# Ternary weight making in an 8-core attention and BitLinear kernel: moved ahead of the second projection batch, from VectorE to ScalarE, and through device memory

## The reference

```python
xn = layernorm(x)
# attention part, per sequence
q, k, v = xn @ Wq, xn @ Wk, xn @ Wv
gq = sum_s(q * softmax(q * SCALE, -1))
p  = gq * k
gk = sum_s(p * softmax(p * SCALE, -1))
attn = q + (gk * v) @ Wr
# feed-forward part: 8-bit activations, ternary weights
scale_w = 1 / clip(mean(abs(w)), 1e-5)
wq = clip(round(w * scale_w), -1, 1) / scale_w        # for w_gate, w_up, w_down
ffn = bitlinear(silu(bitlinear(xn, w_gate)) * bitlinear(xn, w_up), w_down)
y = x + attn + ffn
```

## Time and profile before

| | us |
|---|---|
| timed runs, all (2) | 5378.8 and 5394.5, median 5386.6 |
| profiled execution, its own time | 5350.1 |
| its span, slowest core (core 5) | 5348.5 |
| quickest cores (1 and 3) | 5265.2 |
| DVE busy | 3306.7 (62%) |
| PE busy | 2379.1 (44%) |
| ACT busy | 1899.7 (36%) |
| POOL busy | 60.7 (1%) |

### The profile page before, as it was taken

The page is one execution under the profiler, slowest core; times in us unless marked ns, Lnnn a source line. Parts: engine busy times, 40 slices in busy tenths (PEclk is TensorE's granted clock), DMA queues, the critical chain, the costliest instruction groups (busy, mean ns, idle before and its releaser), DMA issues.

```text
span 5348.5 us, 37244 instructions; the slowest of 8 cores (5265.2 to 5348.5 us)
## 1 busy us (share of the span) xinstructions
PE 2379.1 (44%) x10182; PEld 1037.9 (19%) x10182; DVE 3306.7 (62%) x3647; ACT 1899.7 (36%) x2114; POOL 60.7 (1%) x117
## 2 busy tenths in 40 slices
PE   1443413444100044434444444444444228888888
PEld 0111101111000021212212112112112014433333
DVE  3777657777557767787777777777777701111111
ACT  1222213333000035565565555555555501111111
POOL 1000000000000000000000000000000000000000
PEclk9666656666555567777767777677677558877777
DMA  4222203332233310000000000000000132221121
GB/s 86 79 77 69 75 0 104 108 108 83 84 114 118 113 38 12 20 20 20 20 10 20 20 20 20 20 10 20 20 20 18 34 102 89 85 89 71 73 82 40
DMA packets 85712, 296.02 MB, mean 55 GB/s; under 512 B 9728, under 2 KB 9728, under 8 KB 77312
## 3 DMA queue, kind: packets, MB, share of 16 engines
q1 hardware_dynamic: 32256, 134.23, 7.2%
q10 hardware_dynamic: 39168, 117.46, 6.7%
q0 software_dynamic: 14080, 41.95, 3.2%
HBM read 209.72 MB, written 92.27 MB: 56 GB/s over the span
## 4 chain that ended last, share of the span: by engine, by line
DVE 37%; PE 28%; ACT 17%; issue 9%; DMA 7%; DVEq 1%; ACTq 1%; POOL 0%; SPq 0%; POOLq 0%
ACT rA L685 10%; DVE fl L688 9%; PE PB L626 6%; DVE lh L372 6%; PE PC L629 5%; PE PC L826 5%; PE PA L826 5%; DVE lh L369 3%; PE PB L812 3%; DVE stat L647 3%; PE PT L796 2%; ACT z_hqT L800 2%; DMA wdT_sb<-swdT 2%; ACT f_g L635 2%; DVE fl L694 1%
## 5 line engine op out<-in xcount | busy, mean ns | idle before, releaser
L626 PE MATMUL PB<-wgT_sb,f_xiT 128*128 128x512 bf16 x2048 | 863.7, 422 | 1252.3 <-ACT f_g L635 1185.1
L685 ACT ACTIVATE rA<-fl,cbias 128x1024 bf16<-128x1024 f32 x512 | 588.0, 1148 | 439.0 <-DVE fl L675 284.6
L688 DVE SCALAR_TENSOR_TENSOR fl<-rA,fl 128x1024 f32<-128x1024 bf16 x512 | 627.3, 1225 | 162.9 <-ACT rA L685 162.5
L694 DVE SCALAR_TENSOR_TENSOR fl<-rB,fl 128x1024 f32<-128x1024 bf16 x512 | 625.0, 1221 | 14.6 <-ACT rB L691 12.8
L691 ACT ACTIVATE rB<-fl,cbias 128x1024 bf16<-128x1024 f32 x512 | 586.9, 1146 | 16.9 <-DVE fl L694 15.0
L626 PEld LDWEIGHTS PB<-wgT_sb,f_xiT 128*128 128x128 bf16 x2048 | 218.2, 107 | 1573.4 <-issue 1385.6
L629 PE MATMUL PC<-wuT_sb,f_xiT 128*128 128x512 bf16 x1024 | 468.9, 458 | 0.0
L629 PE MATMUL PA<-wuT_sb,f_xiT 128*128 128x512 bf16 x1024 | 389.4, 380 | 0.0
L635 ACT ACTIVATE f_g<-PB,cgv 128x512 f32<-128x512 f32 x256 | 167.9, 680 | 543.6 <-PE PC L629 531.6
L372 DVE TENSOR_TENSOR lh<-lh,lh 128x1024 f32<-128x1024 f32 x256 | 313.7, 1225 | 27.3 <-DVE lh L369 0.9
L487 PE MATMUL P<-p_w,p_rep 128*128 128x512 bf16 x64 | 37.5, 585 | 596.6 <-DVE p_w L484 566.5
(11 more groups left out here) (129 smaller groups left out, 3480.1 us busy)
## 6 DMA issues: line engine op xcount, KB each, us to landing
shqT<-f_hq SPq DMA_DIRECT2D x32, 1024.0 KB, 4.5
z_hq<-shqT SPq DMA_DIRECT2D x32, 1024.0 KB, 5.5
wf<-wgT ACTq DMA_DIRECT2D x48, 512.0 KB, 3.7
wf<-wuT ACTq DMA_DIRECT2D x48, 512.0 KB, 3.6
wf<-wdT ACTq DMA_DIRECT2D x48, 512.0 KB, 3.6
xbuf<-x SPq DMA_DIRECT2D x32, 512.0 KB, 4.3
sacc<-accs SPq DMA_DIRECT2D x32, 512.0 KB, 2.9
z_acc<-sacc ACTq DMA_DIRECT2D x32, 512.0 KB, 6.3
```

The source lines that it names most:

```text
L626: last = te.matmul(gps, lhsT, wgT_sb[:, k * I + jj * 512:k * I + (jj + 1) * 512], start=(k == 0), stop=(k == 7))
L685: o("scalar", (lambda j=j, scale=scale: lambda s: s.activation(rA[:], fl1[:], AF.Relu, scale=scale, bias=cbias[:, j:j + 1]))(), reads=[fl1 ...
L688: o("vector", (lambda cc=cc, op1=op1: lambda v: v.scalar_tensor_tensor(fl1[:], rA[:], cc, fl1[:], ALU.min, op1))(), reads=[rA_b], writes=[ ...
L694: o("vector", (lambda cc=cc, op1=op1: lambda v: v.scalar_tensor_tensor(fl2[:], rB[:], cc, fl2[:], ALU.min, op1))(), reads=[rB_b], writes=[ ...
```

## The change

passA is done in batch 0's projections altogether, with six items a step in place of two, and the three means follow there. passB then runs earlier: one item behind each of batch 0's softmax tiles (16 items), and five items behind each step of batch 1's projections (80 items in 16 steps; the last two steps have none). Batch 1's second softmax has no passB any more.

What an item does is changed as well. Two ACT instructions compute sign(w*scale - 0.5) into tstA and sign(w*scale + 0.5) into one of two buffers tern_st, both bf16; DVE adds them in bf16, which gives -2, 0 or 2 (the factor 0.5 goes into the scales, L534 of before). The result goes to device memory for all three matrices, on POOL for even items and ACT for odd ones; loads are on ACT for even items and POOL for odd ones, as before. The pieces stand in the order gate, up, down in place of down, up, gate.

The up and gate weights are loaded into SBUF from there, on SP, in 1 MB pieces: 14 of 16 are issued ahead of batch 1's second softmax, and the last two, whose place wgT_hi overlaps that softmax's buffers, behind it. The gate weights lie in two buffers for that, wgT_lo and wgT_hi. In the down stage only addresses change (wdT_sb and the tiles beside it trade places).

```diff
+    swgT_h = nc.dram_tensor("swgT", [D, I], BF16, kind="Internal").ap()
+    swuT_h = nc.dram_tensor("swuT", [D, I], BF16, kind="Internal").ap()
...
+    bm5, bm5_b = sb("bm5", [128, 1], F32, 19.875)
+    bp5, bp5_b = sb("bp5", [128, 1], F32, 19.9375)
...
-    wf32_t, wf32_bl = sb("wf32", [128, 2 * D], F32, 197.125, nbuf=2)
+    wf32_t, wf32_bl = sb("wf32", [128, 2 * D], F32, 197.375, nbuf=2)
     wf32 = [wf32_t[:, i * D:(i + 1) * D] for i in range(2)]
-    wabs, wabs_b = sb("wabs", [128, D], BF16, 205.25)
+    wabs, wabs_b = sb("wabs", [128, D], BF16, 205.375)
...
-    ternA, ternA_b = sb("ternA", [128, D], F32, 127.5)
-    ternA2, ternA2_b = sb("ternA2", [128, D], F32, 37.125)
-    wgT_sb, wgT_sb_b = sb("wgT_sb", [128, 8 * I], BF16, 69.125)
...
+    tstA, tstA_b = sb("tstA", [128, D], BF16, 191.375)
+    tern_st_t, tern_st_bl = sb("tern_st", [128, 2 * D], BF16, 193.375, nbuf=2)
+    tern_st = [tern_st_t[:, i * D:(i + 1) * D] for i in range(2)]
+    wgT_lo, wgT_lo_b = sb("wgT_lo", [128, 6 * I], BF16, 69.125)
+    wgT_hi, wgT_hi_b = sb("wgT_hi", [128, 2 * I], BF16, 117.125)
...
+    wdT_sb, wdT_sb_b = sb("wdT_sb", [128, 32 * D], BF16, 133.125)
...
+            if drip is not None:
+                drip()
+
+    passB = ([("wg", k) for k in range(32)] + [("wu", k) for k in range(32)]
+             + [("wd", k) for k in range(32)])
+
+    def emit_passB(idx):
+        nm, k = passB[idx]
+        slot = idx % 2
+        if nm == "wd":
+            src = wdT_h[k * 128:(k + 1) * 128, :]
+            dst = swdT_h[k * 128:(k + 1) * 128, :]
+            ridx, dst_b = 10, swdT_b[k]
+        else:
+            w_hh = wgT_h if nm == "wg" else wuT_h
+            s_hh = swgT_h if nm == "wg" else swuT_h
+            src = w_hh[(k // 4) * 128:(k // 4 + 1) * 128, (k % 4) * D:(k % 4 + 1) * D]
+            dst = s_hh[(k // 4) * 128:(k // 4 + 1) * 128, (k % 4) * D:(k % 4 + 1) * D]
+            ridx = 8 if nm == "wg" else 9
+            dst_b = (swgT_b if nm == "wg" else swuT_b)[k]
+        o("scalar" if idx % 2 == 0 else "gpsimd",
+          (lambda src=src, slot=slot:
+           lambda s: s.dma_start(out=wf32[slot], in_=src))(),
+          writes=[wf32_bl[slot]], dma=True)
+        o("scalar", (lambda slot=slot, ridx=ridx: lambda s: s.activation(
+            tstA[:], wf32[slot], AF.Sign, scale=wstat[:, ridx:ridx + 1],
+            bias=bm5[:, 0:1]))(),
+          reads=[wf32_bl[slot], wstat_b, bm5_b], writes=[tstA_b])
+        o("scalar", (lambda idx=idx, slot=slot, ridx=ridx: lambda s: s.activation(
+            tern_st[idx % 2], wf32[slot], AF.Sign, scale=wstat[:, ridx:ridx + 1],
+            bias=bp5[:, 0:1]))(),
+          reads=[wf32_bl[slot], wstat_b, bp5_b], writes=[tern_st_bl[idx % 2]])
+        o("vector", (lambda idx=idx: lambda v: v.tensor_tensor(
+            tern_st[idx % 2], tern_st[idx % 2], tstA[:], ALU.add))(),
+          reads=[tstA_b, tern_st_bl[idx % 2]], writes=[tern_st_bl[idx % 2]])
+        o("gpsimd" if idx % 2 == 0 else "scalar",
+          (lambda idx=idx, dst=dst: lambda s: s.dma_start(
+              out=dst, in_=tern_st[idx % 2]))(),
+          reads=[tern_st_bl[idx % 2]], writes=[dst_b], dma=True)
+
+    pb_i = [0]
+
+    def drip_passB(n):
+        for _ in range(n):
+            if pb_i[0] < len(passB):
+                emit_passB(pb_i[0])
+                pb_i[0] += 1
+
+    p1_batch(0, 6)
...
-    o("vector", lambda v: v.tensor_scalar_mul(wstat[:, 12:15], wstat[:, 4:7], -1.0),
+    o("vector", lambda v: v.tensor_scalar_mul(wstat[:, 12:15], wstat[:, 4:7], 0.5),
...
-    passB = ([("wd", k) for k in range(32)] + [("wu", k) for k in range(32)]
-             + [("wg", k) for k in range(24)] + [("wg", k) for k in range(24, 32)])
...
-        tA, tA_b = (ternA2, ternA2_b) if (nm == "wg" and k >= 24) else (ternA, ternA_b)
-        o("vector", (lambda slot=slot, ridx=ridx, tA=tA: lambda v: v.tensor_scalar(
-            tA[:], wf32[slot], wstat[:, ridx:ridx + 1], 0.5, ALU.mult, ALU.is_ge))(),
-          reads=[wf32_bl[slot], wstat_b], writes=[tA_b])
-        o("vector", (lambda slot=slot, ridx=ridx, oap=oap: lambda v: v.tensor_scalar(
-            oap, wf32[slot], wstat[:, ridx:ridx + 1], -0.5, ALU.mult, ALU.is_le))(),
-          reads=[wf32_bl[slot], wstat_b], writes=[tgt_b])
-        o("vector", (lambda oap=oap, tA=tA: lambda v: v.tensor_tensor(
-            oap, oap, tA[:], ALU.subtract))(),
-          reads=[tA_b, tgt_b], writes=[tgt_b])
-        if nm == "wd":
-            o("scalar", (lambda k=k: lambda s: s.dma_start(
-                out=swdT_h[k * 128:(k + 1) * 128, :], in_=wabs[:, 0:D]))(),
-              reads=[wabs_b], writes=[swdT_b[k]], dma=True)
-
...
-    for i2, t in enumerate(range(NTB, NT)):
+    for t in range(NTB):
         p2_tile(t)
-        drip_passB(6, 88)
+        drip_passB(1)
+    o("vector", lambda v: v.tensor_copy(gk_s[:, 0:D], gkbc[:]),
+      reads=[gkbc_b], writes=[gk_s_b])
+    o("vector", lambda v: v.memset(gqbc[:], 0.0), writes=[gqbc_b])
+    o("vector", lambda v: v.memset(gkbc[:], 0.0), writes=[gkbc_b])
+
+    p1_batch(1, 0, drip=lambda: drip_passB(5))
+    drip_passB(len(passB))
+
+    def wu_load(kk):
+        o("sync", (lambda kk=kk: lambda s: s.dma_start(
+            out=wuT_sb[:, kk * I:(kk + 1) * I],
+            in_=swuT_h[kk * 128:(kk + 1) * 128, :]))(),
+          reads=[swuT_b[kk * 4 + j] for j in range(4)],
+          writes=[wuT_sb_b], dma=True)
+
+    def wg_load(kk):
+        tgt, tb = (wgT_lo, wgT_lo_b) if kk < 6 else (wgT_hi, wgT_hi_b)
+        c0 = kk * I if kk < 6 else (kk - 6) * I
+        o("sync", (lambda kk=kk, tgt=tgt, c0=c0: lambda s: s.dma_start(
+            out=tgt[:, c0:c0 + I],
+            in_=swgT_h[kk * 128:(kk + 1) * 128, :]))(),
+          reads=[swgT_b[kk * 4 + j] for j in range(4)],
+          writes=[tb], dma=True)
+
+    for kk in range(8):
+        wu_load(kk)
+    for kk in range(6):
+        wg_load(kk)
+    for t in range(NTB, NT):
+        p2_tile(t)
     o("vector", lambda v: v.tensor_copy(gk_s[:, D:2 * D], gkbc[:]),
       reads=[gkbc_b], writes=[gk_s_b])
-    drip_passB(len(passB), len(passB))
+    wg_load(6)
+    wg_load(7)
...
-                last = te.matmul(gps, lhsT,
-                                 wgT_sb[:, k * I + jj * 512:k * I + (jj + 1) * 512],
-                                 start=(k == 0), stop=(k == 7))
+                wg_sl, _ = wg_ap(k, jj * 512, (jj + 1) * 512)
+                last = te.matmul(gps, lhsT, wg_sl, start=(k == 0), stop=(k == 7))
```

More of the change, by code:

```diff
@@ L128, in build_nc @@
     swdT_b = [Buf("swdT%d" % k) for k in range(32)]
+    swgT_b = [Buf("swgT%d" % k) for k in range(32)]
+    swuT_b = [Buf("swuT%d" % k) for k in range(32)]
     allocs = []
@@ L203, in build_nc, with wg_ap @@
     p2_rep, p2_rep_b = sb("p2_rep", [128, 128], BF16, 127.15625)
-    ternA, ternA_b = sb("ternA", [128, D], F32, 127.5)
-    ternA2, ternA2_b = sb("ternA2", [128, D], F32, 37.125)
-    wgT_sb, wgT_sb_b = sb("wgT_sb", [128, 8 * I], BF16, 69.125)
+    tstA, tstA_b = sb("tstA", [128, D], BF16, 191.375)
[3 more added lines that the diff above has]
+    wgT_hi, wgT_hi_b = sb("wgT_hi", [128, 2 * I], BF16, 117.125)
     wuT_sb, wuT_sb_b = sb("wuT_sb", [128, 8 * I], BF16, 133.125)
+    def wg_ap(k, off0, off1):
+        if k < 6:
+            return wgT_lo[:, k * I + off0:k * I + off1], wgT_lo_b
+        return wgT_hi[:, (k - 6) * I + off0:(k - 6) * I + off1], wgT_hi_b
     f_xi_t, f_xi_bl = sb("f_xi", [128, 2 * D], BF16, 37.125, nbuf=2)
@@ L263, in build_nc @@
     o("vector", lambda v: v.memset(halfv[:], 0.5), writes=[halfv_b])
+    o("vector", lambda v: v.memset(bm5[:], -0.5), writes=[bm5_b])
+    o("vector", lambda v: v.memset(bp5[:], 0.5), writes=[bp5_b])
     for j in range(8):
@@ L494, in p2_tile, with p1_batch @@
               reads=[P7_b], writes=[gkbc_b])
-    def p1_batch(bi, rate):
+    def p1_batch(bi, rate, drip=None):
         base = bi * NTB
@@ L509, in p1_batch @@
             drip_passA(rate)
-    p1_batch(0, 2)
-    for t in range(NTB):
-        p2_tile(t)
-    o("vector", lambda v: v.tensor_copy(gk_s[:, 0:D], gkbc[:]),
-      reads=[gkbc_b], writes=[gk_s_b])
-    o("vector", lambda v: v.memset(gqbc[:], 0.0), writes=[gqbc_b])
-    o("vector", lambda v: v.memset(gkbc[:], 0.0), writes=[gkbc_b])
-    p1_batch(1, 4)
+            if drip is not None:
+                drip()
+    passB = ([("wg", k) for k in range(32)] + [("wu", k) for k in range(32)]
+             + [("wd", k) for k in range(32)])
@@ L573, in build_nc @@
-    pb_i = [0]
-    def drip_passB(n, limit):
-        for _ in range(n):
-            if pb_i[0] < limit:
-                emit_passB(pb_i[0])
-                pb_i[0] += 1
-    for i2, t in enumerate(range(NTB, NT)):
-        p2_tile(t)
-        drip_passB(6, 88)
+    for t in range(NTB):
+        p2_tile(t)
+        drip_passB(1)
+    o("vector", lambda v: v.tensor_copy(gk_s[:, 0:D], gkbc[:]),
+      reads=[gkbc_b], writes=[gk_s_b])
+    o("vector", lambda v: v.memset(gqbc[:], 0.0), writes=[gqbc_b])
```

(2 more changed lines are left out.)

41 lines of the change are left out of this document (11 added, 30 removed).

## The result

The changed kernel takes **5657.6 us** (median of 11 runs) against 5310.4 us before (10 runs): the ratio is 1.0644, with a 95% interval of 1.0582 to 1.0706. Of 5310 us that is 342, and the medians differ by 347; the forecast sum was +359. The profiled execution took 5687.3 us.

A forecast was written before the change was run, and what follows sets the result against it. DVE, nearly gapless, was taken to set the pace of a batch 1 projection step, with ACT slack. Terms +59 + 11 + 649 - 360 = +359 on the profiled 5350.1 us, plus 18 for timed runs, gave 5727 us; range 5590 to 5840.

The forecast's parts named there:

- The ring of five items: Batch 1's projections: each item runs load, two Signs, add, store, with nothing of the next starting early; +649 us.
- the 8.7 and 8.8: Batch 1's projections, inside a step: an odd item costs 8.7 us, an even item 8.8, from add to add.
- the 71 and 80: Batch 1's projections: steps alternate near 71 and 80 us, as they begin with an even or odd item.
- 5.22: Batch 1's projections: microseconds from an even item's load issue on ACT until its data are used.
- The last softmax: Batch 1's second softmax, without passB: 517.3 us falls to 157.8, including 13 us to the first gate matmul; -360.
- passA: Batch 0's projections, six items a step instead of two: 39 us for late ACT plus 20 for slower weight loads, +59.
- The rate part: Batch 0's projections: two more items than the four shown make ACT 2.8 us late in 14 steps, 39 us.
- the first two steps slow the loading of wq, wk and wv: Start of batch 0's projections: eight more passA loads each slow a projection weight load by 2.5 us, +20.
- The first softmax: Batch 0's second softmax: one passB item per tile costs only DVE's add, 0.69 us (upper end 1.23), 16 times: +11.
- Rival (c), tables: Sign is not in ACT's loaded function table; extra table loads cost 41 us, at worst 82; about 5790; chance 0.09.
- (a): Batch 1's projections: loads hidden, only Signs and add remain, 3.2 us an item, 222 instead of 649; 5300 us; chance 0.06.
- (b): Batch 1's projections: ACT's work fits under DVE's quantisation, leaving 80 adds, 55 us; total -235, 5133 us; chance 0.04.

The follow-up runs named there:

- the experiment: Kernel before with passA at six items a step, all in batch 0's projections, and the means ahead of batch 0's second softmax: 5314.8 against 5281.7 us.

## Why the prediction held, point by point

- **The ring of five items (+649, measured +637)** is shown: parting loads from stores, from either side, brings 245 to 362 us. The 8.56 us between adds answer to the 8.7 and 8.8, and steps of 72.4 and 79.8 us (from 957.20, 1029.61 and 1109.44) to the 71 and 80; over the batch those that begin even take 67 to 72 us and those that begin odd 77 to 82.
- **Inside the ring** the numbers were less good than the sum, and that they agree in the mean is luck: inside a step an even item took 8.05 us and an odd one 9.08 (means of 32 each), where I had 8.8 and 8.7. An ACT load took 4.40 us from issue to use where I had 5.22, a POOL load 4.64 where I had 4.45, and it was issued 0.73 behind the start of the store where I had 0.53.
- **Where the 5.22 came from**: it was read at a place where a second load and a store were under way beside the load. ACT's loads in that softmax of before took 4.96 us to landing where both were (median of 15) and 3.72 where neither was (22); inside the change's steps, with a store alone beside them, 3.85 (32). This is a sorting of loads and no experiment. The Trainium skill, DMA: Bandwidth & Descriptors, on queues, rings and completion order, says that the increment of a DMA's semaphore lands after the earlier writes of that DMA engine. I had read it as making every load behind a store late; the 3.85, against 3.57 for the eight ACT loads here with no store beside them, show 0.3 us of that (0.6 as means), not the 1.6 that I took. What held the loads was that they were issued late.
- **The last softmax (-360, measured -361)** held. From its last add to the first gate matmul it took 14.5 us where I had 13, by another path than I had: the first exposed 1 MB load landed 5.9 us after its issue at 2214.61, and then the second load (2220.55 to 2226.69) and f_xi's (2220.96 to 2227.41) went side by side. I had put them one behind the other, and f_xi's took 6.5 us where it took 2.6 in the kernel before, with no weights under way.
- **passA (+59, measured +32 without the means)** is the term that failed. The rate part held: L442 comes 2.4 us late in a step as a mean of 14 instead of 2.8, and the experiment gives +33 in all. The part "the first two steps slow the loading of wq, wk and wv", +20, does not exist: the first Kst cast comes at 129.0 us, before at 131.0. Twelve passA loads lie in that stretch in place of four, and the last of the 24 weight loads landed at 115.7 us, before at 117.4. The slower load of the earlier trace rows was one of few, with the last load of wq (46.16 to 51.63) beside it too, and I had multiplied its excess by eight. ACT around the end of a late step, where the sixth item (431.81) pushes the casts and L442 behind DVE's maximum, which began at 431.64:

```profile
431.81 1.06 ACT L309 ACTIVATE wabs<-wf 128x1024 bf16<-128x1024 f32 x1 [2.62 <-DMA wf<-wuT]
...
435.28 0.20 ACT L442 ACTIVATE stat<-stat 128x1 f32<-128x1 f32 x1 [0.51 <-ACT v L434]
```

- **The first softmax (+11, measured +16)**: the add is 691 ns, the lower bound. The Trainium skill, VectorE: DVE Perf Modes, in its tier table, gives an all-bf16 tensor_tensor two elements a cycle, and the trace agrees (691 ns against 1.23 us for the add with an f32 tile). What was missing are odd items. The load that POOL issued at 722.10 was used only at 729.02, 6.9 us later, and DVE idled 1.58 us before its add:

```profile
722.10 0.54 POOL L547 DMA_DIRECT2D wf<-wgT  x1
...
729.02 1.24 ACT L549 ACTIVATE tstA<-wf,bm,wstat 128x1024 bf16<-128x1024 f32 x1 [4.02 <-DMA wf<-wgT]
...
731.50 0.69 DVE L557 TENSOR_TENSOR tern_st<-tern_st,tstA 128x1024 bf16<-128x1024 bf16 x1 [1.58 <-ACT tern_st L553]
```

- **Rival (c), tables**: there are again two table loads, 1283 ns each, the first ahead of the first function and the second before Silu. Sign needed none beside exponential, logarithm and copy.
- **Rivals (a) and (b)** did not happen in the change, yet both mechanisms are real: (a) priced 3.2 us an item, and with the loads on SP the shortest spacings are 3.25 us (its 222 us for the stretch are not reached, 277 are, as late loads make the mean 3.93); (b), the work under the quantisation, forecast 5133 us, but it needed the adds moved into it.
- **The total**: the forecast lies 69 us above the median. Of these the sum is 12 (359 against 347), and 58 the start it was added to: I had put 18 us on top of the profiled 5350, because the two runs shown took longer; with ten runs the median of before is 5310, 40 below the profiled one. The sum, too, is closer than its terms deserve: between the two profiled spans the stages add up to +337, and the forecast's errors of +25 (passA), -5, +12, +1 and -11 cancel in part.

## What to carry to other kernels

In these traces the DMAs of an engine go out in program order, so put no load behind a store, or behind any other instruction of that engine, that waits for a result: what counts is where the load can be issued, not how long it takes, and one line that parts them was worth some 350 us ((1.0644 - 0.9982) x 5282). Work that is moved "into the shadow" of a busy engine must be written between that engine's instructions; in one piece behind them, it pays its whole latency. Price such a move by its ring (result, store, next load, arithmetic, result), and look for each other waiting DMA in the same queue, here the sxi store, which was worth 116 us.

## What the hardware showed that I had not expected

- ACT issues a DMA ahead of arithmetic that precedes it in the program (1658.70, before a Sign that began at 1659.75), but not ahead of arithmetic that waits: it left 0.09 us after the Sign at 1658.61 that had waited, and with the stores on SP an ACT load left at 1246.65, behind a Sign that had waited 24.72 us.
- An add put between two dependent DVE instructions cost less than its length: 5 adds of 0.68 us lengthened a step by 2.20 us (37.33 - 35.13), 0.44 each. Without it, L384 starts 1.34 us after L387 (1233.13 to 1234.47), 0.11 after its end; with it, the add starts 1.14 after L387, before its end, and L384 0.61 after the add (1230.60, 1231.74, 1232.35), together 1.75 and so 0.41 more; the fifth add, behind the quantisation, makes 1.14 us into 1.75.
- POOL's loads took longer beside a busy DVE: a median of 4.9 us for wgT in the first softmax and 6.9 to use in the one shown, 4.0 to 4.5 in batch 1, where DVE mostly waits. Whether DVE's work, or the stores that go out just ahead, makes the difference was not tried. Nor is a late landing POOL's alone: with the loads on SP, where mostly another load was under way beside them, the medians in batch 1 are 4.2 to 5.8 us.
